# Two transformer layers of 16 short sequences on one core: engine loops written as pairs and stages, then as streams of steps in an order from a table

## The reference

```python
x = x + _L0_xattn_ref(_layernorm(x), ctx_1024, ...)            # local cross attention, 16 heads of 8
x = x + _L0_attn_ref(_layernorm(x), ...)                       # RWKV-like recurrence over 32 steps
x = x + _L0_ffn_ref(_layernorm(x), ...)                        # 8 experts, top 2, all computed; shared expert
x = x + _L1_xattn_ref(_layernorm(x), ctx_1024, ctx_1024, mask) # full cross attention with a mask
x = x + _L1_attn_ref(_layernorm(x), ...)                       # linear attention and a GELU feed-forward
x = x + _L1_ffn_ref(_layernorm(x), ...)                        # 16 experts, top 1, capacity 32
```

```python
scores = einsum('bhqd,bhkd->bhqk', qh, kh) * scale + mask * NEG
weights = softmax(scores); out = einsum('bhqk,bhkd->bhqd', weights, vh)
```

## Time and profile before

| | us |
|---|---|
| median of three runs | 326.56 (323.68 to 328.05) |
| the profiled execution: time | 319.62 |
| the profiled execution: span, first to last instruction | 317.6 |
| PE busy / DVE busy / ACT busy | 281.4 / 189.4 / 139.3 |
| mean granted clock of TensorE | 0.936 |
| first scores of the full attention | 108.2 |
| last output matmul of the full attention ends | 256.9 |
| first dispatch matmul of the last half of experts | 299.6 |

### The profile page before, as it was taken

One profiled execution on the slowest core, in us unless ns is written; L12 is line 12 of the kernel. 1 busy time (PEld: TensorE's weight loads), 2 busy tenths in 40 slices (PEclk: granted clock), 3 DMA queues, 4 the chain that ended last, 5 costly groups with the idle time before them and its releaser, 6 DMA issues.

```text
span 317.6 us, 5216 instructions
## 1 busy us (share of the span) xinstructions
PE 281.4 (89%) x1990; PEld 181.5 (57%) x1990; DVE 189.4 (60%) x507; ACT 139.3 (44%) x296; POOL 27.9 (9%) x47
## 2 busy tenths in 40 slices
PE   8998999687988866997989999988899959979996
PEld 6325876166877543554566555454556528667766
DVE  3555265877443487975454668776753774742572
ACT  1215533454650374579713677375368800132130
POOL 4000000000030400013001200000100001010000
PEclk9999999999997999599565999999969989999999
DMA  7999290000019100050005000000000294000001
GB/s 288 427 439 398 66 198 3 0 1 2 0 43 417 70 1 2 0 134 0 0 3 132 3 0 2 2 1 0 2 0 2 91 436 169 1 2 0 0 2 35
DMA packets 3400, 26.79 MB, mean 84 GB/s; under 512 B 432, under 2 KB 1456, under 8 KB 1840
## 3 DMA queue, kind: packets, MB, share of 16 engines
q1 hardware_dynamic: 3376, 26.47, 23.0%
HBM read 26.20 MB, written 0.26 MB: 83 GB/s over the span
## 4 chain that ended last, share of the span: by engine, by line
PE 41%; DVE 9%; issue 5%; ACT 5%; POOL 1%; POOLq 0%; DVEq 0%; ACTq 0%
PE bank L1344 8%; PE bank L1334 8%; PE bank L1359 5%; PE bank L1498 3%; PE bank L1128 1%; PE bank L1305 1%; PE bank L1562 1%; PE bank L1417 1%; PE bank L1383 1%; PE bank L1553 1%; PE bank L1535 1%; PE bank L1442 1%; PE bank L1118 1%; ACT L601 1%; ACT work_sb L601 1%
## 5 line engine op out<-in xcount | busy, mean ns | idle before, releaser
L601 ACT ACTIVATE work_sb<-work_sb,small_sb 128x512 f32<-128x512 f32 x48 | 34.7, 722 | 45.6 <-DVE small_sb L941 45.4
L941 DVE CUSTOM_DVE_ANT_0 work_sb<-bank,mask_sb 128x512 f32<-128x512 f32 x48 | 31.9, 689 | 17.3 <-PE bank L1334 16.8
L1334 PE MATMUL bank<-k_sb,work_sb 32*128 32x512 f32 x128 | 40.2, 706 | 0.6 <-DVE small_sb L941 0.5
L1344 PEld LDWEIGHTS bank<-early_sb,work_sb 128*128 128x128 f32 x192 | 22.4, 151 | 30.3 <-issue 16.6
L1344 PE MATMUL bank<-early_sb,work_sb 128*128 128x128 f32 x192 | 33.9, 305 | 1.1 <-ACT work_sb L608 1.1
L374 POOL TENSOR_TENSOR rstd_sb<-veps_sb,minus_half_sb 128x2 f32<-128x2 f32 (+1 forms) x13 | 10.1, 774 | 214.9 <-DVE veps_sb L701 171.3
L1359 PE MATMUL bank<-work_sb,v_sb 128*32 128x128 f32 x512 | 22.6, 300 | 4.5 <-DVE otmp_sb L922 2.8
L608 ACT COPY work_sb<-bank 128x512 f32<-128x512 f32 x40 | 22.7, 568 | 6.6 <-PE bank L1344 6.6
L1498 PE MATMUL bank<-early_sb 128*128 128x256 f32 x98 | 25.0, 397 | 0.0
L950 DVE COPY work_sb<-bank 128x512 f32<-128x512 f32 x24 | 16.5, 688 | 11.5 <-PE bank L1344 9.8
L1498 PEld LDWEIGHTS bank<-early_sb 128*128 128x128 f32 x98 | 18.9, 203 | 3.1 <-issue 0.8
(11 more groups left out here) (234 smaller groups left out, 454.3 us busy)
## 6 DMA issues: line engine op xcount, KB each, us to landing
ctx_sb<-moe_w SPq DMA_DIRECT2D x1, 4096.0 KB, 12.0
k_sb<-moe_w SPq DMA_DIRECT2D x1, 4096.0 KB, 13.6
ctx_sb<-ctx SPq DMA_DIRECT2D x3, 1024.0 KB, 14.1
late_sb<-late SPq DMA_DIRECT2D x1, 2895.0 KB, 20.6
mask_sb<-ctx_tok SPq DMA_DIRECT2D x1, 2048.0 KB, 12.3
v_sb<-ctx_tok SPq DMA_DIRECT2D x1, 2048.0 KB, 26.9
mask_sb<-mask SPq DMA_DIRECT2D x4, 512.0 KB, 8.1
mask_sb<-mask SPq DMA_DIRECT2D x8, 256.0 KB, 4.6
```

The lines of the kernel that those rows point to most:

```text
L601: s.activation(sc[u % NSC], sc[u % NSC], ACT.Exp, bias=smin[:, u:u + 1], scale=-1.0, accum_out=rsum[:, u:u + 1]).then_inc(sig("p1_ready"), 1)
L941: v.tensor_tensor_reduce(sc[u % NSC], bank[SB[u % NS]][:, :], mask[:, KEYS * b:KEYS * (b + 1)], MASK_BIG, 3e38, ALU.add, ALU.min, smin[:, ...
L1334: mm(bank[SB[u % NS]][:, :], qc[b][r, :], k1[r, KEYS * b:KEYS * (b + 1)], start=True, stop=True)\
L1344: last = nc.tensor.transpose(bank[2 + u % NT][:, P * k:P * (k + 1)], sc[u % NSC][:, P * k:P * (k + 1)], wt("ident"))
```

## The change

Every engine's work is cut into streams of short steps: L (local), P (projections), a and b (small stages of half 0 and 1), S (scores; minimum; exponential), T (transposes; copies), V (outputs; taking the heads), c and d (linear stages of half 0 and 1, d with the experts). A step is what stands between two `yield`s, and the padding is gone. `run` calls them in the order of a string per engine. On PE the first S stands after all of L, P and a, and after b's recurrence and second norm; c begins after S9; the first d stands behind V15, and c's feed-forward and gate are interleaved with d.

- The scores of a batch are four matmuls one after the other, from the four strips of 32 rows, into four banks (0, 1, 2, 5). They wait once, for the four minima of the batch before.
- `outputs` is one step per batch. The transposes have banks 3 and 4, the output bank 6; the stages of half 0 and half 1 have separate banks (5 and 7 for X, 6 and 7 for Y), norm counters and tiles where they now overlap. The score tiles are eight instead of four and lie in the tile of the context; the transposed tiles stay eight.
- All 64 copies of transposed tiles are ScalarE's (`BY_DVE = ()`). VectorE takes eight of the 32 projections instead of four (`LAST = 16`).
- ScalarE writes the hidden tiles of the top-2 feed-forward with Identity, and one SiLU over 1024 columns and one over 256 follow right behind the logarithm. In half 0 the GELU is one instruction over 1024 columns.
- Reciprocals of 256 columns are cut in two of 128.
- W1 is fetched behind the last transposes, after W2; the second and third part of the mask wait for `x1_new`, the counter of half 1.
- `keep_warm` and its calls are gone; the seven matmuls at the start stay.

```diff
-PAIRS = 2 * UNITS // 2
-LATE_OUT = 3
-ROUNDS = PAIRS + LATE_OUT + 1
-LINEAR = 2 * (2 * (HB - 1) + LATE_OUT + 3)
+TURNS = {
+    "PE": (
+        "L2 P L3 P L2 P L2 P L3 P L P5 L P L8 P L2 a L2 P L2 P L2 a L2 P L a3 P4 L P L8 P L P a b P3 a3 P a b "
+        "P2 b2 P3 a P a4 b a2 b2 S b T2 b T S T S V T2 S b T2 b T2 S b T2 V b2 T2 S V T b T2 b T2 S V T4 V T2 "
+        "S T2 V T2 S T2 V T S T c T2 V T2 S T c T V T2 S T V T3 c S T c T V T c T S T V c T2 S T c T2 V c T2 "
+        "c T2 S V c T3 V T2 c V c d c d c d6 c d c d3 c d27 "),
...
+    "ACT": (
+        "L2 P6 L P a P4 L8 P L P2 a P a2 L a P2 a2 P a L8 P L P2 a6 b a2 b2 P b P b2 P b a b3 S2 b2 S T2 S b2 "
+        "T b T S4 T2 S2 T2 S2 T2 S3 T2 S5 T2 S T b T2 S T S T S2 T2 S T2 S T2 S2 T2 S T2 S2 T S T S T S T S "
+        "T2 S2 T2 S2 T2 S2 T2 S3 T2 S T c T S T S2 T S T S c4 T2 S2 T2 S2 T S2 T2 S2 T2 S T2 S2 T2 S T S T2 "
+        "c6 d c d4 c2 d13 "),
...
-        SB = (0, 1, 7)
-        NS, NT, NSC, NPT = len(SB), 2, 4, 8
+        SB, TB, OB1 = (0, 1, 2, 5), (3, 4), 6
+        NSC, NPT = 8, 8
...
-        BY_DVE = (1, 4, 7)
+        BY_DVE = ()
...
+        def run(engine, **streams):
+
+            for turn in TURNS[engine].split():
+                for _ in range(int(turn[1:] or 1)):
+                    next(streams[turn[0]], None)
...
             sp.wait_ge(sig("s1_ready"), 2 * UNITS)
             sp.dma_start(k1[:, :], w2_d).then_inc(sig("w2_in"), 16)
+            sp.wait_ge(sig("pT_ps"), 2 * UNITS)
+            sp.dma_start(ctx[:, :], w1_d).then_inc(sig("w1_in"), 16)
...
                 act.wait_ge(sig("w_ready"), h + 1)
                 s.activation(fr[4], fr[3], ACT.Ln).then_inc(sig("ln_ready"), 1)
+                act.wait_ge(sig("hid_ready"), 5 * h + 5)
+                s.activation(hid4[h], hid4[h], ACT.Silu).then_inc(sig("silu_ready"), 1)
+                s.activation(hid[h][4][0:H0, :], hid[h][4][0:H0, :], ACT.Silu).then_inc(sig("silu_ready"), 1)
+                yield
...
+            def scores():
+
+                for b in range(BATCH):
+                    if b == 0:
+                        pe.wait_ge(sig("o0_ready"), 2)
+                    else:
+                        pe.wait_ge(sig("s1_min"), GROUPS * b)
...
+                    for g in range(GROUPS):
+                        r = slice(32 * g, 32 * g + 32)
+                        mm(bank[SB[g]][:, :], qc[b][r, :], k1[r, KEYS * b:KEYS * (b + 1)], start=True, stop=True)\
+                            .then_inc(sig("s1_ready"), 1)
+                    yield
+
+            def turns():
+
+                for u in range(2 * UNITS):
+                    pe.wait_ge(sig("p1_ready"), u + 1)
+                    if u < 2:
+                        name, n = taker(len(PROJ) - 2 + u)
+                    else:
+                        name, n = copied(u - 2)
                     pe.wait_ge(sig(name), n)
+                    for k in range(KT):
+                        last = nc.tensor.transpose(bank[TB[u % 2]][:, P * k:P * (k + 1)], sc[u % NSC][:, P * k:P * (k + 1)], wt("ident"))
+                    last.then_inc(sig("pT_ps"), 1)
+                    yield
...
-            def keep_warm(n):
-
-                for _ in range(n if alone[0] else 0):
-                    mm(bank[2][:, 0:256], wt("ident"), wt("wv0")[:, 0:256], start=True, stop=True)
```

More of the change, by code:

```diff
@@ L1106, in _ @@
+            run("DVE", L=local(), P=projections(), a=small_stages(0), b=small_stages(1), S=least(), T=copies(), V=take_heads(),
+                c=linear_stages(0), d=experts())
         @block.tensor
@@ L1154, in local, with projections @@
-            def local(h, stages, pace):
-                step = 0
-                def headsum(n):
-                    if n == 2:
-                        pe.wait_ge(sig("o0_ready"), 1)
-                    for c in range(4 * n, 4 * n + 4):
+            def projections():
+                for i, (kind, b) in enumerate(PROJ):
+                    pe.wait_ge(sig(f"ctx_in{piece_of(b)}"), 16)
+                    if kind == "v":
+                        pe.wait_ge(sig("late_in"), 16)
+                        if b >= HB:
+                            pe.wait_ge(sig("z_ps"), BATCH)
+                    if i >= 2:
+                        name, n = taker(i - 2)
+                        pe.wait_ge(sig(name), n)
+                    dst = bank[3 + i % 2]
+                    if kind == "k":
+                        last = mm(dst[:, :], wt("wk1"), ctx[:, KEYS * b:KEYS * (b + 1)], start=True, stop=True)
+                    else:
+                        for k in range(KT):
+                            at = KEYS * b + P * k
+                            last = mm(dst[:, P * k:P * (k + 1)], ctx[:, at:at + P], wt("wv1"), start=True, stop=True)
+                    last.then_inc(sig("proj_done"), 1)
+                    yield
@@ L1337, in turn @@
[L1337 to L1349 removed]
+                for at in (0, 2):
+                    if h and at:
+                        pe.wait_ge(sig("hsc_ready"), 6)
+                    for n in range(2):
+                        last = mm((B, A)[at // 2][:, HTOK * n:HTOK * (n + 1)], wt("spread", E0)[:, P * (at + n):P * (at + n + 1)],
+                                  cfT[h], start=True, stop=True)
+                    last.then_inc(sig("spread_ps"), 1)
+                    yield
@@ L1350, in outputs @@
+            def outputs():
+                for b in range(BATCH):
                     for j in range(GROUPS * b, GROUPS * (b + 1)):
@@ L1364, in full @@
-            def full(second, first):
-                for w in range(ROUNDS):
-                    if w < PAIRS:
-                        scores(w)
-                    if 1 <= w <= PAIRS:
-                        turn(2 * (w - 1))
-                    if LATE_OUT <= w < PAIRS + LATE_OUT:
-                        outputs((w - LATE_OUT) // 2, (w - LATE_OUT) % 2)
-                    if w <= PAIRS:
-                        beside(2 * w, second, first)
-                        if w:
-                            turn(2 * w - 1)
-                        beside(2 * w + 1, second, first)
@@ L1446, in linear_stages @@
-                yield
-                keep_warm(2)
-                pe.wait_ge(sig("ffh_ready"), 4 * h + 4)
+                for i in range(2):
+                    wait_norm(h)
+                    if i and not h:
+                        pe.wait_ge(sig("ffh_ready"), 2)
+                    for n in (2 * i, 2 * i + 1):
+                        last = mm((B, A)[i][:, HTOK * (n % 2):HTOK * (n % 2 + 1)], wt("w1")[:, P * n:P * (n + 1)], lnT[:, c],
+                                  start=True, stop=True)
+                    last.then_inc(sig("ffh_ps"), 1)
+                    yield
@@ L1509, in _ @@
-            turn_norm(X, range(TT))
-            for _ in range(1, PRE):
-                projection()
-            wait_norm()
-            mm(Y[:, :], wt("wq0"), lnT[:, :], start=True, stop=True).then_inc(sig("q0_ps"), 1)
-            local(0, iter(()), pace_local)
-            stages = small_stages(0)
-            local(1, stages, pace_local)
-            alone[0] = True
-            finish(stages)
-            alone[0] = False
-            first = linear_stages(0)
-            full(small_stages(1), first)
@@ L1567, in constants @@
+            run("PE", L=local(), P=projections(), a=small_stages(0), b=small_stages(1), S=scores(), T=turns(), V=outputs(),
+                c=linear_stages(0), d=experts())
 def constants():
```

1336 lines of the change are left out of this document (613 added, 723 removed), and 4 rows, old and new, of the table TURNS.

## The result

The changed kernel takes 275.25 us (median of four runs, 274.33 to 276.69) against 325.12 us of the kernel before on the same chip: 0.8545 of its time, 95% interval 0.8487 to 0.8603. I had forecast 301 us, with 284 as the lower end. The direction was right, the size was not: 26 us of the gain were missing from my sum. The ratios here compare only the faster of the two states in which a kernel can execute, so they are not the quotients of the medians beside them.

The account below looks back on a forecast made before the run. The attention was taken as bound by TensorE's own work, not by a wait. 108 us to the first scores, 112 of attention and 73 after it made 293 of span, 295 in all, scaled to 301 us; range 284 to 326.

Parts of the forecast that it names:

- Up to the first scores: Stretch before the full attention: the first scores stay at 108 us, between 102 and 114.
- Scores: Full attention: four strips cost a pair's price, so the group of scores halves, 40.2 to 20.1 us.
- The rest of the attention: Full attention: TensorE's work 102.0 us after work moved out, plus 10 us idle (3 to 25), 112 us.
- ScalarE level with TensorE: Attention loop: ScalarE, with all copies, 4.7 us a batch against TensorE's 4.56, so the two bound together.
- Behind the last output: From the last output to the end, linear stage and experts: 60.7 us becomes 72.7, bounds 61 to 85.
- the term for the clock: After the last output: without fillers the lower clock adds 10 us, and 2 in the experts (0 to 22).
- the terms for reciprocals, woven chains and moved work: After the last output: reciprocals no longer waiting minus 3 us; half 0's feed-forward, GELU and gate woven in plus 4 us.
- The scale: Whole kernel: profiled execution 6.9 us under the median, so 295 us was scaled proportionally to 301.
- Strips in two pairs: Attention scores: four strips do not run together, price 20 us, 321 us in all; chance 0.10.
- Order out of step: Fixed engine orders: one late step stops all streams behind it, plus 21 us, 322 us in all; chance 0.15.
- Lower clock in the attention: Attention: the clock falls and stays down, 3.6 us more a batch, 351 us in all, slower; chance 0.10.
- the better case: Whole kernel: the tail keeps its clock (-12), scores cost the lower end (-3), 286 us; chance 0.07.

## Why the prediction was wrong, step by step

**Up to the first scores.** Forecast 108, measured 111.7, inside 102 to 114. TensorE's work came out as said (61.5 us for an even 60.2), VectorE's at 55.8 for 59. What I left out is that this stretch loses its clock with its fillers: I had taken off their time and nothing more. The granted clock is 0.62 from 98 us to the first scores; with eight fillers in the right waits the scores start at 107.8, and in the kernel before they start 2.6 us later without fillers. Either is about the size of the 3.7 us.

**Scores.** Priced at 20.1 us less, measured 21.0 less. A pair's price for four strips was right. The whole number has some luck: the 40.2 us of before held pairs at the lower clock, which this price halved and did not take out. The Trainium skill's 3.07 for four row tiles (page "TensorE: Matmul & The Clock Gate", Part 3), by which I had 1.3 us a batch, does not show: 1.07 us to the next start, so four strips run fully side by side.

**The rest of the attention: the step that failed.** I had TensorE at 102.0 us and 10 us of idle time, 112 in all; it was 88.7 and 6.2, so 13.3 and 3.8 us of the 17.1 that were missing here. The sum kept the half-clock stretches of before as they were ("still with the half-clock stretches in it"). They were 0.11 of 148.7 us by the mean clock, twice that in length, 33 us; now it is 0.05 of 94.9, 9.5 us long. Half the length is lost at most, 16 and 5 us, so up to 12 us. The groups show that it is less. I had scores, transposes and outputs at 88.0 us together; they measured 75.6 (19.2, 38.3 and 18.1), 12.4 less. At clock 1.00 the transposes of before took 18.11 us for 112 records (177 to 229) and the outputs 8.37 for 208; now it is 17.85 for 121 and 7.57 for 224 (158.7 to 197.6), the outputs of four strips. So at the same clock too these steps became cheaper, by 0.014 and 0.006 us a record, 3.6 and 3.3 us over all. The clock is then an estimated 3.4 us on the transposes, 1.2 on the outputs and 1.2 on the scores. In the new order two transposes often follow each other directly, and so do the two halves of an output:

```profile
155.39 1.09 PE L1299 MATMUL bank<-early_sb,ctx_sb 128*128 128x128 f32 x8
156.41 1.08 PE L1315 MATMUL bank<-work_sb,v_sb 128*32 128x128 f32 x32
```

Two transposes take 1.02 us to the next start, where I had 2 x 0.59; an output of a batch takes 1.01 (152.28 to 153.29), where I had 2 x 0.57. So two terms of the sum were mis-sized, by about 6 us each in these groups: the clock, and the price of a transpose and of an output, which I had taken from steps that stood apart. The clock depended on the order and the strips, and I carried it over as a constant. Of the 53.8 us by which the attention got shorter, four strips are 26.0 (about 16 their own time, 10 the clock). The other 27.8 are everything else in the change, since the kernel with pairs has it all: 17.4 us less of TensorE's busy time (132.2 to 114.8) and 10.4 less of its idle time (16.5 to 6.1). No run takes the order apart from the moved work, the banks or the batched SiLU. The copies give nothing by themselves in the kernel before.

**ScalarE level with TensorE.** Right: 88 us forecast, 87.0 measured, TensorE at 88.7, and copies 1.18 us apart:

```profile
162.14 0.59 ACT L567 COPY work_sb<-bank 128x512 f32<-128x512 f32 x1
...
163.32 0.60 ACT L567 COPY work_sb<-bank 128x512 f32<-128x512 f32 x1
```

That a further cut of TensorE's part would show nothing was nearly right (4.2 us off gave 1.4). I did not see the third limit, the minima between two batches' scores.

**Behind the last output.** Forecast 72.7, measured 66.2. With fillers it is 58.6, against my 60.7 without the term for the clock: the terms for reciprocals, woven chains and moved work sum right to 2 us, but no run tests them one by one, so that they cancel may be luck. The clock's term was 12 and is 7.6. I had the lower clock for nearly all of the part before the experts; by the mean clock of 0.79 it held for 28 of the 66.2 us. With half 0's steps not woven in it was 0.69, so they keep it up in a part of the stretch. What I costed at plus 4 us, the weaving, is worth 21 to 38 us against a chain that stands alone. My sum did not need that number, because it started from a kernel in which half 0's chain already ran beside other work.

**The scale.** The profiled run of before was 6.9 us under its median, and I scaled it up. That of the changed kernel, 274.81 us, stands at its median. This is 6 of the 26 us; 17.1 are the attention and 6.5 the stretch behind it, less 3.7 at the start. That the profiled execution of before was a short one is chance, and so is this part of the error.

**The rivals.** Strips in two pairs: not so, and the price of 20 us was near (27 measured). Order out of step: waits of transposes in the attention sum to 2.1 us, not 15; but the run with a quarter of the copies back on VectorE shows how close it is, at 18 us. Lower clock in the attention: the reverse. The Trainium skill's rule that full speed does not engage for transposes (same page, Part 4) was the ground for it. From 158.7 to 197.6 us the clock reads 1.00, with transposes for 46% of the time (17.85 of 38.9 us), so the trace disagrees as far as 46% go. Between 149.6 and 158.7 us, where little else is woven in, they reach 60% (5.44 of 9.07), also at 1.00. I gave the better case 0.07 with the right first cause, the clock, in the wrong place: the tail lost it and the attention won it.

## What to carry to other kernels

When a change reorders TensorE's work, take the half-clock stretches of the trace out of the base before adding up, and put them back as a range; here they went from 33 to 9.5 us, and no run gave a rule for it. Price steps in the neighbourhood that they will have: two transposes together took 1.02 us, apart 1.18. Price an overlap of dependent chains by what a chain alone takes, waits and lower clock included, and not by busy times. Put fillers only into a wait, behind the last matmul that others need: here eight of them brought the first scores 3.6 us forward, and 27, ten of them in front of a product that was due, set them 4.1 us back.

## What the runs showed of the hardware

Four matmuls on row strips of 32 partitions, 512 columns each, cost 1.07 us to the next start, hardly more than one matmul of 512 columns (1.01); at the lower clock the same group takes 2.0 us (the changed kernel's first scores, from 111.72 to 113.74). A filler of 256 columns takes 0.43 us at full clock in a run of ten (4.32 us to the next start), and 0.49 over the 41 of the last stages (20.0 us). And the granted clock can read 1.00 for 39 us with transposes for 17.85 of them on TensorE. TensorE's mean clock in the stretch behind the attention went from 0.79 to 1.00 with 41 matmuls that nobody reads, and the stretch from 66.2 to 58.6 us.
